# Cross-attention scores: three products out of two 128-row and two 64-row matmuls per pair of banks

## The reference, cut to what matters

```python
q = (x @ Wq).reshape(B, N, H, D).transpose(0, 2, 1, 3)
kv = (context @ Wkv).reshape(B, M, 2, H, D).transpose(2, 0, 3, 1, 4)
k, v = (kv[0], kv[1])
attn = jnp.einsum('bhnd,bhmd->bhnm', q, k) * SCALE
attn = jnp.where(mask[:, None, :, :], attn, -jnp.inf)
attn = jax.nn.softmax(attn, axis=-1)
out = jnp.einsum('bhnm,bhmd->bhnd', attn, v)
```

## Time and profile before

| | |
|---|---|
| time, median of 3 runs | 842.32 us (841.49 to 844.99) |
| profiled execution, first to last instruction | 848.8 us |
| PE busy, of that span | 755.1 us (89%) |
| DVE busy | 653.2 us (77%) |
| ACT busy | 457.9 us (54%) |
| POOL busy | 138.9 us (16%) |
| mean granted TensorE clock | 0.954 |

### The profile page before, as it was taken

One profiled execution on the slowest core, in us unless ns is written; L12 is line 12 of the kernel. 1 busy time (PEld: TensorE's weight loads), 2 busy tenths in 40 slices (PEclk: granted clock), 3 DMA queues, 4 the chain that ended last, 5 costly groups with the idle time before them and its releaser, 6 DMA issues. The chain is left out here.

```text
span 848.8 us, 19493 instructions
## 1 busy us (share of the span) xinstructions
PE 755.1 (89%) x6136; PEld 681.1 (80%) x6137; DVE 653.2 (77%) x1619; ACT 457.9 (54%) x922; POOL 138.9 (16%) x246
## 2 busy tenths in 40 slices
PE   3988799999999999999999999999986416999996
PEld 2778689989889899898898998988975314999995
DVE  5984647788888888888888888888878465777773
ACT  2544626566566665666666656666665432334332
POOL 3100110120211201202112012021120410222221
PEclk9999989999999999999999999999978856999999
DMA  6242110010101000000010000000123260111110
GB/s 211 70 138 70 47 29 7 24 29 15 29 12 28 28 6 28 24 16 28 12 28 28 6 28 24 17 28 12 54 113 99 101 235 26 36 39 39 37 33 15
DMA packets 25525, 39.32 MB, mean 46 GB/s; under 512 B 3086, under 2 KB 18704, under 8 KB 25360
## 3 DMA queue, kind: packets, MB, share of 16 engines
q1 hardware_dynamic: 23232, 33.02, 12.5%
q0 software_dynamic: 2256, 5.83, 2.0%
HBM read 28.82 MB, written 10.41 MB: 46 GB/s over the span
## 5 line engine op out<-in xcount | busy, mean ns | idle before, releaser
L1076 ACT ACTIVATE ps_cross<-flip 128x512 f16<-128x512 f32 (+1 forms) x256 | 125.0, 514 | 116.5 <-PE flip L795 91.0
L1318 DVE TENSOR_TENSOR ps_cross<-flip,ps_cross 128x512 f16<-128x512 f32 (+1 forms) x256 | 145.0, 583 | 24.8 <-ACT ps_cross L1076 20.4
L795 PE MATMUL flip<-ident,exp_cross 128*128 128x128 f32 (+1 forms) x832 | 131.8, 282 | 9.9 <-DVE ps_cross L1318 6.5
L1277 ACT ACTIVATE exp_cross<-exp_cross,xneg 128x1024 f32<-128x1024 f32 (+1 forms) x128 | 122.7, 960 | 19.2 <-DVE xneg L1492 19.1
L784 PE MATMUL scores<-keys_cross,qt 128*128 128x402 f32 x512 | 127.6, 372 | 5.3 <-DVE xneg L1492 3.5
L795 PEld LDWEIGHTS flip<-ident,exp_cross 128*128 128x128 f32 (+1 forms) x832 | 95.8, 143 | 18.1 <-DVE ps_cross L1318 8.3
L672 PE MATMUL scores<-keys_self,u_tile 128*128 128x512 f32 x384 | 102.2, 403 | 6.4 <-issue 4.9
L806 PE MATMUL cross_out<-vals_cross,ps_cross 128*128 128x128 f16 (+1 forms) x832 | 102.5, 224 | 5.5 <-issue 4.9
L771 PE MATMUL flip<-vals_self,ps_self 128*128 128x256 f32 x768 | 103.8, 289 | 0.0
L806 PEld LDWEIGHTS cross_out<-vals_cross,ps_cross 128*128 128x128 f16 (+1 forms) x832 | 76.4, 101 | 28.3 <-issue 20.4
L771 PEld LDWEIGHTS flip<-vals_self,ps_self 128*128 128x128 f32 x768 | 96.7, 194 | 0.0
(11 more groups left out here) (207 smaller groups left out, 1189.2 us busy)
## 6 DMA issues: line engine op xcount, KB each, us to landing
w_stage<-W SPq DMA_DIRECT2D x8, 1024.0 KB, 5.4
u_dram<-u_out SPq DMA_DIRECT2D x4, 1024.0 KB, 5.9
u_tile<-u_dram SPq DMA_DIRECT2D x16, 256.0 KB, 2.7
mask_tile<-mask SPq DMA_DIRECT2D x16, 200.1 KB, 2.4
rows<-rows_dram SPq DMA_DIRECT2D x19, 130.0 KB, 2.1
x_all<-x SPq DMA_DIRECT2D x4, 512.0 KB, 5.8
x_tile<-x SPq DMA_DIRECT2D x16, 128.0 KB, 2.0
b_row<-b SPq DMA_DIRECT2D x1, 2048.0 KB, 8.9
```

Of the source, the lines that this page charges most:

```text
L795: tr = pe.transpose(flip[0:rows, bank(use), n * P:(n + 1) * P], exp_cross[:, h % 2, m * P:m * P + rows], ident[:, :])
L1076: return act.activation(out, in_, ACT.Copy, **kw)
L1277: act.activation(exp_cross[:, h % 2, cols], exp_cross[:, h % 2, cols], ACT.Exp, bias=xneg[:, h % 2, 1:2], scale=-1.0, accum_out=xden[:, ha ...
L1318: return dve.tensor_tensor(out, full, hi, ALU.subtract)
```

## The change

Keys: `keys_cross` shrinks to one copy. ACT still writes the high part into all 128 partitions; DVE overwrites one half of the partitions with the low part, the upper half (64 to 127) in key blocks 0 and 2, the lower half in 1 and 3. Queries: ACT writes q, scaled, as float32, each head twice side by side (`q_pair`); the transposes lay q in both halves of the partitions; ACT copies the high part from there to `qt` part 0 and DVE the low part to `qt` part 1. Scores: for each of the two banks one 128-row pass of q high over the mixed keys, then for each bank a 64-row pass of q low over the half that holds k high: rows 0 to 63 for the even bank, 64 to 127 for the odd. So q low times k low is left out. Each 64-row pass raises `cross_scores_ready`, whose counts double. All waits on `qt_ready` are now on `qt_lo`, which DVE raises.

```diff
-    keys_cross = sb("keys_cross", [P, 2, H, MP], F32R, keep)
+    keys_cross = sb("keys_cross", [P, H, MP], F32R, keep)
+    qt = sb("qt", [P, 2, H, P], F32R, keep)
+    apart = sb("apart", [P, H * MP - 2 * H * P], F32, keep)
...
         def cross_scores(j, k, h, half):
             if h == 0 and half == 0:
-                pe.wait_ge(qt_ready, j)
+                pe.wait_ge(qt_lo, j)
...
-            for n in (2 * half, 2 * half + 1):
-                for part in range(2):
-                    mm = pe.matmul(scores[:, n, 0:KB], qt[:, h, :], keys_cross[:, part, h, n * KB:(n + 1) * KB],
-                                   start=(part == 0), stop=(part == 1))
-            mm.then_inc(cross_scores_ready, 1)
+            pair = (2 * half, 2 * half + 1)
+            for n in pair:
+                pe.matmul(scores[:, n, 0:KB], qt[:, 0, h, :], keys_cross[:, h, n * KB:(n + 1) * KB], start=True, stop=False)
+            for n in pair:
+
+                half_rows = slice(HD * (n % 2), HD * (n % 2) + HD)
+                pe.matmul(scores[:, n, 0:KB], qt[half_rows, 1, h, :], keys_cross[half_rows, h, n * KB:(n + 1) * KB],
+                          start=False, stop=True).then_inc(cross_scores_ready, 1)
...
-                copy(qs[:, :, 0, :], flip[:, bank(("xq",)), 0:D].rearrange("p (h d) -> p h d", h=H)).then_inc(qs_hi, 1)
+                act.activation(q_pair[:, :, :, :], flip[:, bank(("xq",)), 0:D].rearrange("p (h d) -> p h d", h=H)
+                               .unsqueeze(2).broadcast_to([P, H, 2, HD]), ACT.Copy, scale=HD ** -0.5).then_inc(q_copied, 1)
...
-                act.activation(qt[:, :, :], flip[:, bank(("qs",)), :].rearrange("p (h s) -> p h s", h=H), ACT.Copy,
-                               scale=HD ** -0.5).then_inc(qt_ready, 1)
+                copy(qt[:, 0, :, :], flip[:, bank(("qs",)), :].rearrange("p (h s) -> p h s", h=H)).then_inc(qt_hi, 1)
...
             if b:
-                dve.wait_ge(qs_hi, j)
-                low(qs[:, :, 1, :], flip[:, bank(("xq",)), 0:D].rearrange("p (h d) -> p h d", h=H),
-                    qs[:, :, 0, :].bitcast(F32)).then_inc(qs_lo, 1)
+                dve.wait_ge(qt_hi, j)
+                low(qt[:, 1, :, :], flip[:, bank(("qs",)), :].rearrange("p (h s) -> p h s", h=H),
+                    qt[:, 0, :, :].bitcast(F32)).then_inc(qt_lo, 1)
             if a:
                 part_max(j, k, 3)
```

More of the change, by code:

```diff
@@ L204, in emit @@
     xt = sb("xt", [P, 2, C, P], F32R, loop)
-    qs = sb("qs", [P, H, 2, HD], F32R, loop)
-    qt = sb("qt", [P, H, P], F32R, loop)
+    q_pair = sb("q_pair", [P, H, 2, HD], F32, loop)
     o_tile = sb("o_tile", [P, H, HD], F32, loop)
@@ L301, in emit @@
     q_ready = sem("q_ready")
-    qs_hi = sem("qs_hi")
-    qs_lo = sem("qs_lo")
+    q_copied = sem("q_copied")
     q_flipped = sem("q_flipped")
-    qt_ready = sem("qt_ready")
+    qt_hi = sem("qt_hi")
+    qt_lo = sem("qt_lo")
     bias_ready = sem("bias_ready")
@@ L825, in flip_queries @@
             for h in range(H):
-                tr = pe.transpose(out[:, h * P:(h + 1) * P], qs[:, h, :, :].bitcast(F32), ident[:, :])
+                tr = pe.transpose(out[:, h * P:(h + 1) * P], q_pair[:, h, :, :], ident[:, :])
             return tr
@@ L877, in body @@
             if b:
-                pe.wait_ge(qs_lo, j)
-                small(("qs",), j, k, qs_lo, j, q_flipped, flip_queries)
+                small(("qs",), j, k, q_copied, j, q_flipped, flip_queries)
             if c:
@@ L1135, in _ @@
                 act.wait_ge(cross_k_ready, H * g + h + 1)
-                copy(keys_cross[:, 0, h, g * KB:(g + 1) * KB], scores[:, h, 0:KB]).then_inc(cross_k_hi, 1)
+                copy(keys_cross[:, h, g * KB:(g + 1) * KB], scores[:, h, 0:KB]).then_inc(cross_k_hi, 1)
                 if g >= 2:
@@ L1197, in body @@
                 if k >= 2:
-                    act.wait_ge(cross_scores_ready, 8 * (j - 1))
-                act.activation(qt[:, :, :], flip[:, bank(("qs",)), :].rearrange("p (h s) -> p h s", h=H), ACT.Copy,
-                               scale=HD ** -0.5).then_inc(qt_ready, 1)
+                    act.wait_ge(cross_scores_ready, 16 * (j - 1))
+                copy(qt[:, 0, :, :], flip[:, bank(("qs",)), :].rearrange("p (h s) -> p h s", h=H)).then_inc(qt_hi, 1)
             if a:
@@ L1429, in _ @@
                 cols = slice(g * KB, (g + 1) * KB)
-                low(keys_cross[:, 1, h, cols], scores[:, h, 0:KB], keys_cross[:, 0, h, cols].bitcast(F32)).then_inc(cross_k_lo, 1)
+                low_rows = slice(0, HD) if g % 2 else slice(HD, P)
+                low(keys_cross[low_rows, h, cols], scores[low_rows, h, 0:KB],
+                    keys_cross[low_rows, h, cols].bitcast(F32)).then_inc(cross_k_lo, 1)
                 if g == 1 and h == H - 1:
@@ L1481, in cross_max @@
         def cross_max(j, k, h, half):
-            dve.wait_ge(cross_scores_ready, 8 * (j - 1) + 2 * h + half + 1)
+            dve.wait_ge(cross_scores_ready, 16 * (j - 1) + 4 * h + 2 * half + 2)
             if half == 0:
```

## The result

The changed kernel takes 885.5 us in the median of 4 runs (884.5 to 887.6), the one before 843.65 (841.5 to 846.2): 1.050 times as long, 95% interval 1.048 to 1.053. The forecast was 877, with 856 to 898 as its range. The time lies close to it, but as the following shows, two of its three large terms were wrong, and their errors nearly cancel.

The account below looks back on a forecast made before the run. PE was taken to set the end, on a critical path alternating with DVE. Wait less passes +17, clock +18, ends +1 and -1.5 made about +35 us on 842.3: 877 us, range 856 to 898.

Parts of the forecast that it names:

- DVE, ready for that at 425.15, waits ... 2.15 us late: Before head 3's values: DVE's last part_max waits behind the low part of qt, starting 2.15 us late; PE waits about 2.1.
- I take the full saving: Scores calls: 64-row passes run side by side, saving 0.19 us a call, 0.93 a round over five calls.
- bound and rival: Scores calls: changing between 128-row and 64-row work empties PE twice, a call 0.13 us longer; rival's chance 0.16.
- What counts of eight calls: In a round, five scores calls lie on PE's part of the critical path; three lie ahead of waits.
- as the forecast said of savings: Scores calls (2,0), (3,0), (3,1): waits for DVE or ACT behind them would take up what they save.
- I take three in four: 18 us: PE's clock falls behind the new gap in three of four of 14 rounds, 1.7 us each: 18 us.
- the very same place of the program: Round 1's 1.87 us PE wait behind the query flips, followed by a clock fall, was taken as the new gap's place.
- falls within the same gap: On PE, cross_flip(3, 2)'s new wait on qt_lo (427.4) falls within the about 2.1 us wait for (3,0).
- +1 for round 1: Round 1: self_exps, already a 1.87 us wait, come about 1.7 later, less four calls: +1 us.
- -1.5 for round 16: Round 16: PE's 1.71 us wait for DVE's low part of qs goes; the new low part still waits: -1.5 us.
- forecast at nothing: Prologue: the low part of the keys keeps 402 columns on half the partitions, so no change in time.
- +17: Rounds 2 to 15: moved work costs 2.15 us, passes give back 0.93, so 1.22 a round, 17 us.

Follow-up runs that it names:

- Experiment 1: Changed kernel with DVE's low part of qt moved behind sneg and the three xcoef steps, ahead of the low part of (3,0): 858.6 us, 1.019 times before.
- 8: Changed kernel with DVE's low part of qt behind the three xcoef steps and 128-row second passes instead of 64-row ones: 850.7 us, 1.009 times before.
- experiment 3: Changed kernel with second passes over all 128 rows instead of 64, all else as changed: 872.1 us, 1.034 times before.
- 2: Kernel before, its queries and keys kept, each call as two 128-row passes and then a 64-row pass a bank: 853.3 us, 1.012 times before.
- experiment 4: Changed kernel with both 64-row passes on the same rows, 0 to 63: 905.2 us in one run.
- Experiment 6: Changed kernel with an unneeded DVE memset each round behind the low part of qt, ahead of the last part_max: 911.9 us in one run.
- second version of experiment 9: Kernel before with only the three xcoef steps moved behind the low part of (3,0) on DVE: 843.3 us, 0.9998 times before.
- experiment 9: Kernel before, xcoef steps behind (3,0)'s low part; first version also xn3 and x1 statistics behind later low parts: 846.8 us; second without these: 843.3.
- experiment 5: Changed kernel with each call's four matmuls alternating 128-row, 64-row, 128-row, 64-row: 974 us, 1.153 times before.

## Why the prediction came out right, and where it was wrong

*"DVE, ready for that at 425.15, waits ... 2.15 us late": right in place and mechanism, a little large.* PE's delay is 1.79 us. DVE's chain from `part_max` to the low part of (3,0) shrank from 2.41 us (425.15 to 427.56) to 2.06 (414.46 to 416.52): the first `xcoef` step takes 0.16 us instead of 0.51. The timelines of DVE and POOL before show what it hung on:

```profile
425.98 0.51 DVE L1528 TENSOR_TENSOR xcoef<-xden 128x4 f32<-128x4 f32 x1
...
424.95 1.53 POOL L598 TENSOR_SCALAR mask_bias<-mask_tile 128x1601 bf16<-128x1601 uint8 x1
```

The step ends at 426.49 and POOL's instruction at 426.48, and so it is in each of rounds 3 to 15: the step lasts 0.23 to 0.84 us and ends within 0.01 of POOL's. In the changed kernel DVE comes 2 us later, and POOL is done:

```profile
412.05 1.53 POOL L599 TENSOR_SCALAR mask_bias<-mask_tile 128x1601 bf16<-128x1601 uint8 x1
```

There the step takes 0.15 or 0.16 in each of these rounds. So the forecast moved as a fixed piece a chain of which 0.35 us was, by these ends, a hold by POOL; no version moves POOL's instruction itself. In experiments 1 and 8, which bring `part_max` back to its early place, the hold is back too, and PE's wait with it. Experiment 1 takes most of the wait away by moving one instruction; experiment 3 shows its worth, 1.71 us a round, 24 us in 14.

*"I take the full saving": wrong in sign.* Forecast -0.93 us a round, measured +0.56 (experiments 2, 3 and 8). The half of the argument that concerned the pair held (experiment 4: 0.19 us). The half that PE could pass from 128-row to 64-row work for nothing did not: the two changes of a call cost 0.16 and 0.14 us, the pair gives back 0.19, so a call is 0.11 dearer (0.93 instead of 0.82). This was bound and rival, priced from the earlier trace rows at 0.13; choosing the other end of a bound that no row of the trace supports cost 21 us.

*What counts of eight calls.* Four calls at 0.11 and the transposes behind them give most of the 0.56. Three of the four calls of the second half are as much dearer, and yet, from the last self values to the next round, the time is 13.36 us (427.50 to 440.86), as before (404.02 to 417.39 on PE's timeline, 13.37): the waits for DVE and ACT there took it up, as the forecast said of savings. With 0.18 more a call (experiment 4) they took up only a part.

*"I take three in four: 18 us": wrong.* Three rounds of 14 lost the clock, about 5 us. The row that the price was read from is not at "the very same place of the program": in round 1 there is no part c, and PE waited ahead of the scores (0,0) for ACT, not ahead of the values of (3,0) for DVE. The gap was taken as one of 2.1 us, beside one of 1.87 in the earlier trace rows; it is two, 0.33 and 1.24, with four transposes between. The step that failed is the sentence that the wait of `cross_flip(3, 2)` "falls within the same gap": it falls in it, but PE then still has that flip to do, which shortens what is left. Experiment 6 shows that with 2.26 us the clock does fall, in eight of 14 rounds, so even a gap of the forecast's size gave less than three in four.

*Ends.* Forecast +1 for round 1, -1.5 for round 16. The first scores start at 126.75 instead of 124.01, +2.7: 1.7 is the longer wait on `self_exps` as forecast (3.53 us instead of 1.87), 1.1 comes from the prologue, which was forecast at nothing. There PE waits 2.28 us for the last low part of the keys instead of 1.52, and the first self scores behind it run in part at a fallen clock (97.29 to 100.71). In round 16, from q to the first scores, 7.2 us (665.52 to 672.71) instead of 8.5: -1.3, near the forecast's -1.5. But the clock was low for 5.2 of these 7.2 us, and for 8.3 of the 8.5 before, which by itself is worth up to 1.5 us; so this agreement says little of the term.

*The sum.* Forecast +17 (30 for the wait less 13 saved by the passes), +18 (clock), -0.5 (ends). Measured 31.8 in the rounds (24 the wait, 8 the passes), about 5 clock, about 1.4 at the two ends: 38, of 42. The remaining 4 aren't placed: the profiled spans, 882.5 and 848.8, differ by only 34, since the profiled execution of before was longer than its usual runs. From the start of round 15 to the end it took 261.7 us. The second version of experiment 9, which has the loop and the time of the kernel before, took 256.1 there, and its span is 841.9. The clock was low for 61.4 us of that stretch in the one and for 58.0 in the other, up to the last few us, which is worth at most 1.7; the rest of the 5.6 is open. The number 877 was good by luck: a clock term 13 us too large and a wait 6 too large stood in for a passes term 21 us too small.

## What to carry to other kernels

Where a step of a chain passes from one engine to another, look at what stands behind it in the new engine's queue: here a 0.69 us instruction at its old place, now waiting for a later event, held the row maximum, the exponentials and the next head, and cost 24 us; its place alone gave 27 us between two versions. A 64-row matmul among 128-row ones pays for the change of shape on both sides, so a pair side by side that saves one step in four does not pay for itself. By these prices longer runs of one shape would be needed; none was tried. An instruction's duration in the trace can hold a wait for another engine: when it is moved, the duration need not move with it. And when a price has no row, keep both ends until something speaks for one.

## What the runs showed of the hardware

- Two float32r matmuls on different halves of the rows and different banks run side by side: 0.45 us for the pair of 402 columns, 0.64 if both use the same rows.
- Going from 128-row to 64-row matmuls, or back, costs 0.14 to 0.18 us at full clock; the weight load of the first matmul in the other shape does not start ahead, but after a pause of 0.19 to 0.27 us.
- DVE's low part of the keys over 64 partitions takes as long as over 128: 0.57 us for 402 columns.
- The granted clock fell behind or within a PE gap of 2.26 us in eight of 14 rounds (experiment 6), and behind gaps of 0.33 and 1.24 us with transposes between in three of 14 in the changed kernel, in four of 14 in experiment 4 and in none in experiment 3, each time for 3.4 us or twice that.
- Ahead of the first self scores, with a dense run of 24 matmuls behind, a PE gap of 2.28 to 2.30 us was followed within 1.5 us by a fall of the clock in seven of the eight versions that have it; the gap of 1.51 or 1.52 us in the four others in none.
- With 128-row and 64-row matmuls alternating (experiment 5), the clock fell 0.9 us behind the 1.24 us gap in every third round and stayed at 0.50 for some 13.6 us, although PE shows as busy throughout; the cause is not settled.
- A 128x4 addition on DVE that starts while POOL's 1.53 us `mask_bias` instruction runs ends together with it: 0.23 to 0.84 us in rounds 3 to 15 of the kernel before, each end within 0.01 us of POOL's. Once POOL is done it takes 0.15 to 0.18 (changed kernel, both versions of experiment 9). The row maxima and low parts of DVE, whose input comes from PE's banks, ran at their usual 0.69 us beside the same POOL instruction.
